# A fused Mamba and mixture-of-experts layer: inverse square roots of the last norm on VectorE or GpSimd

## What is computed

```python
x = layernorm(x + mamba(x))
x = layernorm(x + routed(x) + shared(x))       # the last norm

def layernorm(x, eps=1e-5):
    m, v = mean(x), var(x)                     # over the 128 channels of a token
    return (x - m) / sqrt(v + eps)
```

## Time and profile before

| | us |
|---|---|
| median of 3 runs | 745.13 |
| lowest and highest of them | 744.18, 746.52 |
| the profiled execution, its own time | 745.25 |
| its span in the profile | 743.5 |
| GpSimd busy | 511.8 (69%) |
| VectorE busy | 594.7 (80%) |
| PE busy | 629.1 (85%) |
| ScalarE busy | 444.3 (60%) |
| TensorE clock granted, mean | 0.951 |

### The profile page before, as it was taken

How to read it: one execution, slowest core, us unless ns; L and a number is a source line. 1 busy time by engine, 2 the same in 40 slices (tenths; PEclk the granted TensorE clock), 3 DMA queues, 4 the chain that set the end, 5 groups by cost and what they waited for, 6 DMA issues and landing times.

```text
span 743.5 us, 14720 instructions
## 1 busy us (share of the span) xinstructions
PE 629.1 (85%) x4299; PEld 533.4 (72%) x4299; DVE 594.7 (80%) x1745; ACT 444.3 (60%) x1225; POOL 511.8 (69%) x559
## 2 busy tenths in 40 slices
PE   5987788999999999999999999799987888767700
PEld 4676567777877877878878788688887788657600
DVE  4999979999999999999999989655826544567736
ACT  4885687687687687687787776263313122344727
POOL 1144455688778778777778787747777777788862
PEclk9999999999999999999999999899999999989855
DMA  8641111112122212211212210913423333665317
GB/s 316 200 130 41 30 58 38 51 58 64 51 59 63 55 58 59 57 54 55 62 54 58 61 33 28 307 43 81 118 81 107 94 108 101 193 197 155 109 54 267
DMA packets 62639, 70.76 MB, mean 95 GB/s; under 512 B 10335, under 2 KB 45285, under 8 KB 62304
## 3 DMA queue, kind: packets, MB, share of 16 engines
q1 hardware_dynamic: 52656, 52.79, 24.9%
q0 software_dynamic: 8608, 16.87, 6.6%
q10 hardware_dynamic: 1296, 0.16, 0.1%
HBM read 48.55 MB, written 23.01 MB: 96 GB/s over the span
## 4 chain that ended last, share of the span: by engine, by line
PE 35%; issue 15%; POOL 15%; ACT 13%; DVE 7%; DMA 2%; SPq 1%; POOLq 0%; DVEq 0%; ACTq 0%
POOL returned L589 11%; PE bank L850 5%; PE bank L792 5%; PE bank L783 4%; ACT x L899 4%; ACT rows L991 2%; PE bank L837 2%; PE bank L847 2%; PE bank L766 2%; PE bank L799 2%; PE bank L751 2%; POOL dispatched L648 2%; PE bank L854 2%; PE bank L758 2%; PE bank L814 2%
## 5 line engine op out<-in xcount | busy, mean ns | idle before, releaser
L589 POOL DMA_INDIRECT returned<-xT,slots_in x141 | 142.9, 1014 | 44.1 <-issue 41.8
L648 POOL DMA_INDIRECT dispatched<-rows,row_u x128 | 149.6, 1169 | 31.7 <-issue 31.6
L1107 DVE SCALAR_TENSOR_TENSOR xbcT_area<-raw,conv_w,xbcT_area 128x512 f32<-128x512 f32 x162 | 125.7, 777 | 3.2 <-ACT xbcT_area L965 3.2
L910 ACT ACTIVATE raw<-bank 128x512 f32<-128x512 f32 (+1 forms) x71 | 40.7, 589 | 85.7 <-PE bank L718 82.5
L718 PE MATMUL bank<-xT 128*128 128x128 f32 x564 | 75.6, 290 | 17.6 <-DVE xT L1377 16.8
L936 ACT ACTIVATE zs<-bank 128x256 f32<-128x256 f32 x64 | 24.2, 379 | 110.2 <-PE bank L751 110.2
L1115 DVE TENSOR_TENSOR_SCAN decay_area<-decay_area,ident_heads 128x512 f32<-128x512 f32 x64 | 86.9, 1358 | 0.0
L718 PEld LDWEIGHTS bank<-xT 128*128 128x128 f32 x564 | 70.8, 203 | 20.0 <-DVE xT L1377 17.1
L1388 DVE COPY xT<-bank 128x512 f32<-128x512 f32 (+1 forms) x36 | 24.4, 677 | 65.4 <-DMA returned<-xT,slots_in 51.6
L738 PE MATMUL bank<-xbcT_area,raw 128*128 x564 | 72.9, 286 | 0.8 <-ACT raw L910 0.7
L899 ACT ACTIVATE x<-x,shift,rstd 128x128 f32<-128x128 f32 x128 | 52.1, 480 | 35.0 <-DVE shift L1098 35.0
(11 more groups left out here) (225 smaller groups left out, 1516.4 us busy)
## 6 DMA issues: line engine op xcount, KB each, us to landing
decay_area<-decay_rows SPq DMA_DIRECT2D x64, 256.0 KB, 3.3
slots_in<-dispatched SPq DMA_DIRECT2D x141, 64.5 KB, 2.1
hid<-returned SPq DMA_DIRECT2D x18, 256.0 KB, 3.6
xT<-xT_dram SPq DMA_DIRECT2D x8, 512.0 KB, 8.3
x<-x_dram SPq DMA_DIRECT2D x8, 512.0 KB, 7.7
out_dram<-x SPq DMA_DIRECT2D x16, 256.0 KB, 4.8
xT<-returned SPq DMA_DIRECT2D x14, 256.0 KB, 3.8
returned<-xT,slots_in POOLq DMA_INDIRECT x141
```

The source lines that it names most:

```text
L589: e.indirect_dma_start(returned, bass.IndirectOffsetOnAxis(ap=slots_in[sb_][:, n, D:ROW].bitcast(U32), axis=0), slots_out[b][:, n * P:(n + ...
L648: e.indirect_dma_start(dispatched, bass.IndirectOffsetOnAxis(ap=row_u[t % 2][:, m:m + 1], axis=0), rows[t % 3][:, k, c4, :], None).then_in ...
L1107: e.scalar_tensor_tensor(o, r[:, n:n + W], conv_w[:, k, TAPS - 1 - n:TAPS - n], o, ALU.mult, ALU.add).then_inc(S["conv"])
```

## The change

For the six sets that close beside groups, (0,2) to (10,12), the roots are taken on VectorE: at the start of `by_token(t1)`, 12 instructions of 128 x 8 elements, each waiting for the one before it by a semaphore of its own. An integer shift and a multiply-add on the bits give a first guess (0x5F3759DF - i/2), and three steps of Newton's method y (1.5 - 0.5 v y y) follow, the last one written to `rstd`. The `shift` of both tiles follows at once. GpSimd no longer takes part for these sets. Sets (12,14), (14,15) and (15,16) are as before. `SETS_BESIDE` comes out as 6.

```diff
@@ -32,7 +32,7 @@
     "consts_cast", "w_out_scaled", "rate_negated", "dt_raw_added", "dt_step", "conv", "running", "state",
     "mix", "y_carried", "y_sum", "skip_diag", "gated", "residual", "ln_stats", "shift",
     "logits", "top", "hot", "rows_taken", "shared_added", "w1_scaled", "early_total", "early_table", "table", "slots_turned", "w1_picked",
-    "routed_out", "gate", "routed_added",
+    "routed_out", "gate", "routed_added", "last_rstd",
 
     "rate", "dt_exp", "chunk_decays", "step_decay", "rows_copied", "xbc_raw", "xbc_silu", "z_silu", "xdt", "g_squares", "bt",
     "gT_copied", "x1", "x2", "xn", "xnT_copied", "hidden_silu", "routed_silu", "gate_exp", "second_scaled",
@@ -167,7 +167,11 @@
         return gr - TAIL_FROM if 0 <= gr - TAIL_FROM < TAIL_BESIDE else None
 
 
+
     TAIL_SETS = [(t, t + 2) for t in range(0, NT - 2, 2)] + [(NT - 2, NT - 1), (NT - 1, NT)]
+    SETS_BESIDE = sum(t1 <= TAIL_BESIDE for _, t1 in TAIL_SETS)
+    ROOT_STEPS = 12
+    ROOT_GUESS = 0x5F3759DF
 
     def turns_of(group):
         return [n for n, (c0, c1) in enumerate(TURNS) if STEPS[group][0] <= c0 < STEPS[group][1]]
@@ -333,6 +337,10 @@
         picked = [[a.rearrange("p (c d) -> p c d", c=4) for a in pair] for pair in picked]
 
         fill_row = sb("fill_row", [P, NR], I32)
+
+        carve, _ = carver(y_inside[:])
+        root_v, root_y, root_t = (carve(8) for _ in range(3))
+        root_i = carve(8).bitcast(I32)
         count_i = sb("count_i", [P, 2 * NR], I32)
 
         TPE, TP = EARLY // 8, -(-(SLOT_TILES - EARLY) // 8)
@@ -592,7 +600,7 @@
 
             def last_scales(s):
 
-                for n, (t0, t1) in enumerate(TAIL_SETS):
+                for n, (t0, t1) in enumerate(TAIL_SETS[SETS_BESIDE:]):
                     if t1 == s + 1:
                         on.wait_ge("ln_stats", 8 * (NT + s) + 8)
                         on.wait_ge("shift", NT)
@@ -652,9 +660,6 @@
                     return_rows(n - 2)
             for gr in range(GROUPS_IN_LOOP, GROUPS):
                 return_rows(gr)
-                s = tail_step(gr)
-                if s is not None:
-                    last_scales(s)
             for s in range(TAIL_BESIDE, NT):
                 last_scales(s)
 
@@ -1418,7 +1423,34 @@
                 e.tensor_tensor(pick_v[:], pick_v[:], gden[:].unsqueeze(2).to_broadcast([P, NC, TOP_K]), ALU.mult).then_inc(S["gate"])
 
 
+            def roots(n, t0, t1):
+
+                w, made = 4 * (t1 - t0), ROOT_STEPS * n
+
+                def step(k, instruction):
+                    instruction.then_inc(S["last_rstd"])
+                    on.wait_ge("last_rstd", made + k)
+                of = rstd[:, t0:t1, 0, :]
+                by_tile = lambda a: a[:, 0:w].rearrange("p (t c) -> p t c", c=4)
+                v, half = by_tile(root_v), by_tile(root_t)
+                on.wait_ge("ln_stats", 8 * (NT + t1))
+                on.wait_ge("gate", 1)
+                on.wait_ge("x1", 4 * NT)
+                step(1, e.tensor_scalar(v, mv[:, 4 * t0:4 * t1, 1].rearrange("p (t c) -> p t c", c=4), LN_EPS, None, ALU.add))
+                step(2, e.tensor_scalar(root_i[:, 0:w], root_v[:, 0:w].bitcast(I32), 1, None, ALU.arith_shift_right))
+                step(3, e.tensor_scalar(root_y[:, 0:w].bitcast(I32), root_i[:, 0:w], -1.0, float(ROOT_GUESS), ALU.mult, ALU.add))
+                for k in range(3):
+                    last = of if k == 2 else by_tile(root_y)
+                    step(4 + 3 * k, e.tensor_tensor(half, by_tile(root_y), by_tile(root_y), ALU.mult))
+                    step(5 + 3 * k, e.scalar_tensor_tensor(half, half, -0.5, v, ALU.mult, ALU.mult))
+                    step(6 + 3 * k, e.scalar_tensor_tensor(last, half, 1.5, by_tile(root_y), ALU.add, ALU.mult))
+                for u in range(t0, t1):
+                    e.scalar_tensor_tensor(shift[:, u, 0, :], mv[:, 4 * u:4 * u + 4, 0], -1.0, rstd[:, u, 0, :], ALU.mult, ALU.mult).then_inc(S["shift"])
+
             def by_token(t):
+                for n, (t0, t1) in enumerate(TAIL_SETS[:SETS_BESIDE]):
+                    if t1 == t:
+                        roots(n, t0, t1)
                 if t < NT:
                     b = t % len(picked)
                     on.wait_ge(f"picked{b}", 32 * (t // len(picked) + 1))
```

## The result

The kernel after takes **738.22 us** (median of 5 runs, 736.71 to 740.47) beside 745.13 (5 runs, 744.18 to 746.52): a ratio of 0.9917, 95% interval 0.9900 to 0.9933, or 6.9 us. The forecast was 736.2, in a range of 734.8 to 739.8. The profiled execution is the median one itself: 738.22, with a span of 736.4.

What follows compares the result with a forecast made beforehand. The prediction took GpSimd's issuing of returned rows, with root steps between transfers, as the bound. Five steps removed save 9.6 us, less 0.6 lost waiting for VectorE: 745.25 - 9.0 = 736.2 us, range 734.8 to 739.8.

Steps and rivals of the forecast that it cites:

- GpSimd is the bound: GpSimd, 655 to 720 us: its own order sets the end; five removed root steps give 1.92 us each, 9.6 us.
- The chain on VectorE: VectorE's 12 dependent root steps: 2.55 us a set, ten at 0.20, the shift 0.34, the integer multiply-add 0.22.
- A pair of groups on VectorE: VectorE with shifts and roots needs 13.15 us a pair, GpSimd 10.9; group 27 starts at 658.4.
- The lead: VectorE's head start over GpSimd lasts until group 33, whose late copy loses 0.6 us once; saving 9.0 us.
- Nothing else holds GpSimd: GpSimd's last transfers: no delay beyond the 0.6 us wait for VectorE's copy; otherwise 0.30 us between transfers.
- Transfers keep their 1.056 us: GpSimd's transfers of returned rows, 655 to 720 us: their mean length of 1.056 us stays unchanged.
- The end: Last transfer of returned rows ends near 710.6 us; a tail of 24 us follows unchanged.
- A: VectorE becomes the bound: its root steps cost 0.27 to 0.34 us, time 739.5 to 743.5 us; chance 0.12.
- B: GpSimd's transfers lengthen beside VectorE's chains: ten times 0.3 us, time 739.2 us; chance 0.09.
- C: Something other than the returns sets the end, so the gain is hidden: 745 us; chance 0.04.
- D: Slower: VectorE's chain, from 0.375 us a step, delays group 35's copy; 753 us at 0.5 a step; chance 0.03.

Runs made afterwards that it cites:

- e10: Kernel before with the 12 steps added on VectorE, result to a spare tile, GpSimd's powers kept: 744.09 us, 0.9997 of the kernel before.
- e5: Kernel after, unchanged, on a chip where the kernel before takes 789.05 us: 793.84 us, ratio 1.0054.
- e9: Kernel after, unchanged, on a chip where the kernel before takes 744.69 us: 737.76 us, ratio 0.9900.
- e11: Kernel after with two Newton steps (9 instructions), each woven between independent VectorE instructions: 731.05 us, 0.9820 of the kernel before at 744.69.
- e8: Kernel after with six Newton steps instead of three, 21 instructions a set: 802.28 us, 1.0161 of the kernel before at 789.05.
- e3: Kernel after with two Newton steps instead of three, 9 instructions in a block: 787.38 us, 1.0019 of the kernel before at 785.55.
- e4: Kernel after with all 12 steps, each woven between independent VectorE instructions: 784.99 us, 0.9983 of the kernel before at 785.55.
- e12: Repeat of e4's kernel, all 12 steps woven, on a chip where the kernel before takes 785.61 us: 783.46 us, ratio 0.9969.
- e1: Kernel after, unchanged, one execution for a second trace, on a chip where the kernel before takes 785.55 us: 787.6 us.
- e2: Kernel after without the 12 root steps, both shifts kept: 784.58 us, 0.9984 of the kernel before at 785.55.
- e7: Repeat of e2's kernel, without the 12 root steps: 790.01 us, 1.0008 of the kernel before at 789.05.
- e6: Kernel before, unchanged, run for its trace on a chip where it takes 789.05 us: 789.96 us.
- third series: Runs e9, e10 and e11 on one chip, beside the kernel before at 744.69 us.

## Why the prediction was right, step by step

- **GpSimd is the bound, 1.92 us a root step, five of them.** Right. e10 leaves the load on GpSimd and the time is the old one, and the account of the 41 transfers needs the whole 9.6.
- **The chain on VectorE, 2.55 us a set.** Right in its sum: 2.69, 2.51, 2.69, 2.69 and 2.46 in the kernel after, and 2.42 for the sixth. The dependent steps keep the 0.20 us of the earlier trace rows. One price in it was read wrongly: 0.34 isn't what an integer shift costs. The shift takes 0.17 us where no transfer ends over it (all six of e5), and in the earlier trace rows it ended with the transfer, at 521.79 against 520.81 + 0.97 = 521.78. What was priced as an instruction was a wait for GpSimd's transfer to end, and it can fall on any of the first three steps.
- **A pair of groups on VectorE, 13.15 us; group 27 at 658.4.** Right: 13.05, 13.15 and 13.02, and 658.22.
- **The lead: 0.6 us lost, once, at group 33.** This is the term that was mis-sized. VectorE's copy of group 33 ended at 698.49 where 698.95 was forecast, yet the transfer started at 699.27 and not at once. The sum took a late GpSimd to start when the copy ends; it starts 0.77 to 0.78 us after (698.49 to 699.27, 686.48 to 687.26, in e9 697.30 to 698.07). With shorter transfers GpSimd also wanted group 33 earlier, at 697.7 and not 698.3, and had to wait for group 31 already. That makes 2.5 us instead of 0.6 in the result; in e9 it is 0.5.
- **Nothing else holds GpSimd.** Wrong by 1.7 us: the gap of 2.02 us in group 33, which no row of before shows.
- **Transfers keep their 1.056 us.** They took 1.008 in the result and 1.043 in e9. In both the end comes out within a microsecond of the other (712.34 and 711.42), because with VectorE the slower of the two a shorter transfer only adds to the wait.
- **The end.** From group 33's copy: 698.49 + 0.77, a transfer of 1.12, a gap of 2.02, seven of 1.28 and a last of 0.97 give 712.3, the time measured. The forecast had 710.6, and a tail of 24 us, which held. That the measured time still fell into the range owes something to luck: its high side was made for A and B, and what filled it was the late start and the gap, which neither has as a term.

**The rivals.** A (VectorE's steps cost 0.27 to 0.34) falls by the 0.20 in the rows, but its other half was true in a milder form: VectorE does set the end of this stretch. In the result the waits and the gap cost 4.2 us, in e9 2.2, and in e11 nothing. B (transfers lengthen beside the chain) falls: 0.97 and 0.98 beside it. The ports rule of the Trainium skill ("SBUF — State Buffer", the section on its two separate sides) would have steps and transfers hold each other up. The trace agrees in part, and more than the prediction saw: in four of the six chains one of the first three steps, which read one tensor, was held until the transfer over it had ended, for 0.1 to 0.3 us. The nine steps with two inputs were not. C falls by the tail. D (slower) didn't happen on this chip, and no chain costs its price of 0.375 us a step. But a chain too long for VectorE did what D says on another chip: e5, +0.5%, and e8, +1.6%, at 0.20 us a step, because there VectorE's copies were already late. That GpSimd is the bound, the condition of the forecast, depends on the chip as well as on the kernel.

**Why 6.9 and not more.** Off GpSimd came 9.6 us, and e11 shows that all of it can arrive. In the kernel after, 4.2 us in the result and 2.2 in e9 go back to waits for VectorE's copies and to the gap behind them. VectorE comes late to them because its pair of groups takes 13.1 us, where GpSimd's eight transfers take 8 x (1.008 + 0.30) = 10.5; the chain of 12 dependent steps is 2.5 of the 13.1.

Was it the weaving or the smaller number of steps that cured this in e11? On a chip of 785 us the weaving: nine steps in a block gain nothing (e3), twelve woven ones do (e4, e12). On a chip of 745 us this isn't shown. Nine chained steps take 1.8 to 2.1 us there as well if they behave as in e3 (726.27 to 728.09, 738.42 to 740.51), 0.6 less a set than twelve. By this estimate the copies of groups 31 and 33 would come 1.8 and 2.4 us earlier, which is more than the waits of 0.95 and 1.57 us ahead of them; and the gap was at its full 2.02 us only behind such a wait. So fewer steps alone might have been enough. Neither nine steps in a block nor twelve woven ones, nor a kernel without steps, ran on a chip of 745 us. e11 also enters the stretch 1.4 us earlier than e9 (652.86 and 654.22), but e10 does the same (652.82) without any gain, so I don't count that as its merit.

## What to carry to other kernels

Moving work off an engine that never idles is worth its whole price only until the next engine's results come late; compare the two engines' time per turn, and add what a late start costs beyond the result it waits for. A chain of short dependent instructions is best spread one by one between independent work of the same engine: the same instructions then cost half or less (0.06 to 0.10 us against 0.20). A gain from relieving the bound can be absent on another chip of the same type, so look for a wait on the relieved engine before counting on it. Before an instruction that takes longer than its neighbours is priced by its kind, look whether it ends together with something on another engine.

## What the runs showed of the hardware

- **A late GpSimd wakes late.** From the end of VectorE's copy to the start of the indirect transfer that waited for it: 0.77 to 0.79 us at each of the 88 waits of over 0.35 us for it that the traces of all runs show behind 640 us. The length of that transfer goes with what VectorE does beside it: 1.12 us beside the sums of a tile (687.26, 699.27), 0.97 beside a chain of root steps (e5, 750.67).
- **A short step that reads one tensor can be held until a transfer ends.** In the seven traces with a chain of steps in one block (the result, e1, e3, e5, e8, e9, e10), 17 of the one-input steps (L1439 to L1441 in the kernel after) took 0.25 to 0.45 us instead of 0.17, and each ended within 0.01 us of the end of a transfer. They had started in its last 0.25 to 0.46 us; of the two-input steps in that part none took longer. One of them in e9:

```profile
689.75 1.06 POOL L597 DMA_INDIRECT returned<-xT,slots_in  x1 [0.30 <-issue]
...
690.48 0.32 DVE L1439 TENSOR_SCALAR y_inside<-mv 128x8 f32<-128x8 f32 x1
```

- **A gap at one place of the program.** At the eighth transfer from the end of every kernel, GpSimd can idle with no releaser. It was 2.02 or 2.03 us in all seven traces where the transfer ahead had waited for VectorE (the result, e1, e2, e3, e5, e8, e9); where it hadn't, 1.49 (e4, e12), 1.01 (e7), 0.73 (e6, e10), and nothing beyond the usual 0.30 in the kernel before and e11. It goes with the place in the program. Something that GpSimd must have ready at this point would fit, but no row shows what it is: in the result the packets of the queues named "instruction" nearest ahead of it lie before 697 us, and none lies in the gap itself (700.39 to 702.41).
- **Dependent or not.** An instruction of 128x8 elements takes 0.16 to 0.17 us. In a chain it is 0.20 us start to start; between independent instructions it costs 0.06 to 0.10. The Trainium skill ("VectorE: DVE Perf Modes", the section on the DRAIN that can't be avoided) says that a semaphore after each of a row of copies costs nothing extra, and its rules advise to save instructions and not semaphores. No run here leaves the semaphores out, so none tests that: chained or woven, each step waits for the one before. What the runs add is that the price of the wait depends on the distance. With an independent instruction between the two, half to two thirds of it is gone.
- **Chips differ.** The same kernel took 745 us in the result and the third series, and 785 to 789 on two other chips, all of it in the routed experts' stage, and the ratio of the two kernels went from 0.990 to 1.005. Why is open.
